# Mask addition and row maxima of a graph-attention kernel: one DVE instruction for each head, with negated scores

## The reference, cut to what is computed

```python
bias = jnp.where(adj_matrix > 0, 0.1 * edge_attr_matrix * adjf, -jnp.inf)[:, None]
scores = jnp.einsum('bhqd,bhkd->bhqk', q, k) / np.sqrt(HD) + bias
attn = jax.nn.softmax(scores, axis=-1)
out = jnp.einsum('bhqk,bhkd->bhqd', attn, v)
...
x1 = residual + (out @ wo + bo)
mlp = jax.nn.gelu(n2 @ w1 + b1, approximate=False) @ w2 + b2
...
for k in range(L):                                   # L = 2 layers
    scores = jnp.einsum('bof,bif->boi', q, kk) / SCALE
    scores = jnp.where(mask, -10000000000.0, scores)
    attn = jax.nn.softmax(scores, axis=2)
    attn = jnp.where(mask, 0.0, attn)
    ctx = jnp.einsum('bnd,ed->bne', jnp.einsum('boi,bid->bod', attn, x), Wc[k])
    x = layer_norm(x + ctx, ln_g[k], ln_b[k])
```

## Time and profile before

| | |
|---|---|
| median of 3 runs | 2197.3 us (2193.87 to 2198.27) |
| the profiled execution | 2195.11 us, of which its span is 2193.1 us |
| granted TensorE clock, mean of the span | 0.971 |
| PE busy | 2016.2 us (92%) |
| PEld busy | 1499.2 us (68%) |
| DVE busy | 1721.4 us (78%) |
| ACT busy | 1558.7 us (71%) |
| POOL busy | 961.0 us (44%) |
| chain that ended last, by engine | PE 72%, ACT 13%, DVE 6%, POOL 4% |

### The profile page before, as it was taken

The page is one execution under the profiler, slowest core; times in us unless marked ns, Lnnn a source line. Parts: engine busy times, 40 slices in busy tenths (PEclk is TensorE's granted clock), DMA queues, the critical chain, the costliest instruction groups (busy, mean ns, idle before and its releaser), DMA issues.

```text
span 2193.1 us, 45905 instructions
## 1 busy us (share of the span) xinstructions
PE 2016.2 (92%) x16984; PEld 1499.2 (68%) x16984; DVE 1721.4 (78%) x3397; ACT 1558.7 (71%) x2994; POOL 961.0 (44%) x1304
## 2 busy tenths in 40 slices
PE   5589899999999999999999999999999999999853
PEld 4356677777777777777777777777777777777531
DVE  4566788888888888888888888888888888887422
ACT  2367777777788777777787777777877777777521
POOL 2022344445454454444554544445545444544434
PEclk8799999999999999999999999999999999999976
DMA  3211012222211122222111222222111222210000
GB/s 106 73 49 42 28 45 58 59 59 56 58 49 42 33 59 59 59 59 54 49 42 35 57 58 59 59 54 57 43 39 44 59 59 59 54 50 16 15 10 19
DMA packets 103675, 108.62 MB, mean 50 GB/s; under 512 B 9824, under 2 KB 78432, under 8 KB 103456
## 3 DMA queue, kind: packets, MB, share of 16 engines
q1 hardware_dynamic: 102912, 104.90, 17.9%
q0 software_dynamic: 544, 0.80, 0.2%
HBM read 38.55 MB, written 16.78 MB: 25 GB/s over the span
## 4 chain that ended last, share of the span: by engine, by line
PE 72%; ACT 13%; DVE 6%; POOL 4%; issue 3%; DMA 2%; SPq 1%; DVEq 0%; POOLq 0%; ACTq 0%
PE ps L243 18%; PE ps L245 17%; PE ps L244 17%; PE ps L812 5%; PE ps L972 5%; PE ps L1046 5%; ACT area L483 4%; PE ps L1026 3%; POOL x L403 3%; ACT cs L525 2%; DMA out<-x 2%; ACT area L533 2%; ACT L525 2%; PE ps L965 1%; ACT cq L518 1%
## 5 line engine op out<-in xcount | busy, mean ns | idle before, releaser
L483 ACT ACTIVATE area<-area,nmax 128x128 f32<-128x128 f32 x1024 | 312.5, 390 | 0.8
L243 PE MATMUL ps<-w_h,hid_h 128*128 128x256 f16 x1024 | 279.1, 273 | 6.0 <-POOL hid_l L250 5.1
L245 PE MATMUL ps<-w_h,hid_l 128*128 128x256 f16 x1024 | 279.0, 272 | 0.0
L244 PE MATMUL ps<-w_l,hid_h 128*128 128x256 f16 x1024 | 279.0, 272 | 0.0
L396 POOL TENSOR_TENSOR ve<-mv,eps_cols 128x4 f32<-128x4 f32 x128 | 25.7, 201 | 572.0 <-DVE mv L572 572.0
L250 POOL TENSOR_TENSOR hid_l<-area,hid_h 128x512 f16<-128x512 f32 x128 | 151.8, 1186 | 251.9 <-ACT hid_h L506 251.9
L503 ACT ACTIVATE area<-ps,b_col 128x512 f32<-128x512 f32 x256 | 176.3, 689 | 77.9 <-PE ps L245 76.8
L403 POOL TENSOR_TENSOR x<-xh,cg_row 128x256 f32<-128x256 f32 x128 | 89.0, 728 | 295.7 <-DMA out<-x 272.6
L243 PE MATMUL ps<-rot_h,w_h 128*128 128x512 f16 x512 | 194.4, 380 | 6.2 <-ACT area L503 2.9
L245 PE MATMUL ps<-rot_h,w_l 128*128 128x512 f16 x512 | 194.0, 379 | 0.0
L244 PE MATMUL ps<-rot_l,w_h 128*128 128x512 f16 x512 | 193.9, 379 | 0.0
(11 more groups left out here) (178 smaller groups left out, 6214.0 us busy)
## 6 DMA issues: line engine op xcount, KB each, us to landing
qkS<-qk SPq DMA_DIRECT2D x384, 128.0 KB, 2.4
xin<-in_x SPq DMA_DIRECT2D x32, 512.0 KB, 3.8
adj_in<-in_adj SPq DMA_DIRECT2D x64, 256.0 KB, 2.9
out<-x SPq DMA_DIRECT2D x32, 512.0 KB, 3.9
area<-in_L_gnn_w SPq DMA_DIRECT2D x2, 1024.0 KB, 11.3
area<-in_L_gnn_Wc SPq DMA_DIRECT2D x2, 256.0 KB, 11.3
area<-in_L_gnn_wq SPq DMA_DIRECT2D x1, 256.0 KB, 3.7
area<-in_L_gnn_wk SPq DMA_DIRECT2D x1, 256.0 KB, 4.0
```

Of the source, the lines that this page charges most:

```text
L243: pe.matmul(dst, lh, rh, start=start, stop=False, **kw)
L244: pe.matmul(dst, lh, rl, start=False, stop=False, **kw)
L245: return pe.matmul(dst, ll, rh, start=False, stop=stop, **kw)
L483: last = act.activation(sc[:, b % 2, h], sc[:, b % 2, h], ACT.Exp, bias=nmax[:, b, h:h + 1])
```

## The change

The two DVE steps S and max become one. For each head of A (8 for a graph) and for each graph of C (4 for a layer) DVE issues one instruction that adds the bias to the scores, multiplies by a negative constant, writes the result, and keeps the running minimum of what it wrote. The minimum of the negated scores is the negated maximum that ACT needs; ACT reads the negated scores with scale -1. The steps A.max and C.max leave VECTOR, all else in the lists stays where it was. The semaphores d_max and d_cmax are gone: ACT waits for d_S and d_cS, and these are counted behind the last head. The edge term of biasA is scaled by QK_SCALE ahead, since the addition now comes before the scaling. The line numbers of the changed kernel are one or two higher than those of the kernel before.

```diff
-           "A.wo-1", "A.st-1", "A.S0+0", "C1.S-4", "C1.max-4", "A.xh-1", "A.max0+0", "N.st+1",
+           "A.wo-1", "A.st-1", "A.S0+0", "C1.S-4", "A.xh-1", "N.st+1",
...
-                        need(act, d_max, g, B, b + 1)
+                        need(act, d_S, g, B, b + 1)
                         for h in range(H):
                             last = act.activation(sc[:, b % 2, h], sc[:, b % 2, h], ACT.Exp,
-                                                  bias=nmax[:, b, h:h + 1])
+                                                  bias=nmax[:, b, h:h + 1], scale=-1.0)
...
-                            need(act, d_cmax[l], g, 1, 1)
+                            need(act, d_cS[l], g, 1, 1)
...
-                        dve.scalar_tensor_tensor(adj_f, adj_in[:, :, :], 0.1, adj_in[:, :, :],
+                        dve.scalar_tensor_tensor(adj_f, adj_in[:, :, :], 0.1 * QK_SCALE, adj_in[:, :, :],
...
-                        dve.scalar_tensor_tensor(sc[:, b % 2], psA_heads, 1.0 / QK_SCALE,
-                                                 biasA[:, b].unsqueeze(1).broadcast_to([P, H, P]),
-                                                 ALU.mult, ALU.add).then_inc(d_S, 1)
-                    elif stage == "A" and what[:3] == "max":
-                        need(dve, d_S, g, B, b + 1)
-                        dve.tensor_reduce(nmax[:, b, :], sc[:, b % 2], AX.X, ALU.max, negate=True).then_inc(d_max, 1)
+                        for h in range(H):
+                            last = dve.tensor_tensor_reduce(sc[:, b % 2, h], psA_heads[:, h], biasA[:, b],
+                                                            scale=-1.0 / QK_SCALE, scalar=HIGHEST,
+                                                            op0=ALU.add, op1=ALU.min,
+                                                            accum_out=nmax[:, b, h:h + 1])
+                        last.then_inc(d_S, 1)
...
-                            dve.tensor_tensor(cs[:, l], psC_S, biasC[:, g[1]], ALU.add).then_inc(d_cS[l], 1)
-                        elif what == "max":
-                            need(dve, d_cS[l], g, 1, 1)
-                            dve.tensor_reduce(cmax[:, l], cs[:, l], AX.X, ALU.max, negate=True).then_inc(d_cmax[l], 1)
+                            for b in range(B):
+                                last = dve.tensor_tensor_reduce(cs[:, l, b], psC_S[:, b], biasC[:, g[1], b],
+                                                                scale=-1.0, scalar=HIGHEST, op0=ALU.add,
+                                                                op1=ALU.min, accum_out=cmax[:, l, b:b + 1])
+                            last.then_inc(d_cS[l], 1)
```

More of the change, by code:

```diff
@@ L44 @@
 MASKED = -1e30
+HIGHEST = 3e38
 P_SCALE = 1024.0
@@ L64 @@
 VECTOR = ["Q.k1+0", "A.AV2-1", "A.PT3-1", "A.AV3-1", "C1.xT-4", "A.oT-1", "C0.PV-3", "M.x2-2",
[2 rows of a table removed]
+          "A.wo-1", "A.st-1", "A.S0+0", "C1.S-4", "A.xh-1", "N.st+1",
+          "Q.v1+0", "M.mT-1", "A.S1+0", "M.mC-2", "N.xh+1", "M.lo0-1", "C1.PV-4",
           "A.PT0+0", "C1.st-4", "N.xT+1", "Q.v0+0", "C1.xh-4", "M.lo2-1", "A.S2+0", "C0.xT-2",
[2 rows of a table removed]
+          "Q.k0+1", "C0.st-3", "M.lo4-1", "A.PT1+0", "Q.q0+1", "A.S3+0", "C0.S-2",
+          "A.AV0+0", "M.lo6-1", "Q.q1+1", "Q.mA+1", "A.PT2+0", "C0.xh-3",
           "A.AV1+0"]
@@ L207, in graph_blocks @@
         d_mt, d_mA, d_mC = sem("d_mt"), sem("d_mA"), sem("d_mC")
-        d_S, d_max = sem("d_S"), sem("d_max")
+        d_S = sem("d_S")
         d_PT, d_rec, d_o, d_oT, d_x1 = (sem("d_" + n) for n in ("PT", "rec", "o", "oT", "x1"))
         d_mT, d_lo, d_x2 = (sem("d_" + n) for n in ("mT", "lo", "x2"))
-        d_cT, d_cS, d_cmax = (each_layer("d_" + n) for n in ("cT", "cS", "cmax"))
+        d_cT, d_cS = (each_layer("d_" + n) for n in ("cT", "cS"))
         d_crec, d_csc, d_cy = (each_layer("d_" + n) for n in ("crec", "csc", "cy"))
@@ L521, in iteration @@
                         elif what == "ex":
-                            need(act, d_cmax[l], g, 1, 1)
+                            need(act, d_cS[l], g, 1, 1)
                             for b in range(B):
                                 last = act.activation(cs[:, l, b], cs[:, l, b], ACT.Exp,
-                                                      bias=cmax[:, l, b:b + 1],
+                                                      bias=cmax[:, l, b:b + 1], scale=-1.0,
                                                       accum_out=csum[:, l, b:b + 1])
```

## The result

The changed kernel takes 2200.2 us (2196.7 to 2204.9, 20 runs), the kernel before 2197.2 us (2193.4 to 2199.4, 20 runs) beside it. The ratio is 1.0015, 95% interval 1.0008 to 1.0022: 3 us slower, and within the 0.2% that the prediction called no change. It had forecast 2260 us and 2215 to 2330. The profiled execution of the changed kernel has a span of 2196.3 us, that of the kernel before 2193.1.

A forecast was written before the change was run, and what follows sets the result against it. PE was taken as the bound, losing 2.03 us a period to later bank release: 57 us in the steady part plus 8 at the ends, 65 us on 2195.1, giving 2260 us. Range for 8 in 10: 2215 to 2330.

The forecast's parts named there:

- no change: Rival: PE's stalls hide in something taken for PE-bound that isn't; 2199 us, chance 0.04. Any result within 0.2%: 0.07.
- What bounds the kernel: Steady part: PE is the bound, busy 60.96 of 62.0 us; DVE matters only through when PE's banks are released.
- the term of A.PT1: PE's A.PT1, waiting for A.S2 on DVE, late by 8p - 1.44 = 0.80 us a period.
- three terms: Later bank release for PE: 12p - 2.31 at C1.xW, 8p - 2.06 at A.PT0, 8p - 1.44 at A.PT1.
- The view of the waits: Steady part: PE's idle time is all named by three ACT waits of 0.38, 0.27 and 0.23 us a period.
- The cost of a pair: On DVE, distance p between starts of successive pairs: first half 0.20 plus minimum's read 0.08, p = 0.28 us.
- 28p - 5.81: Lateness of PE summed over the three places, 2.03 us a period, all lost; 57 us over the steady part.
- A.PT0: PE late by 8p - 2.06 = 0.18 us a period, on top of the exps wait; M.mT on DVE not late.
- C1.xW: PE's first matmul into bank 6, waiting for C1.S on DVE, late by 12p - 2.31 = 1.05 us a period.
- DVE's total: DVE's load hardly moves, 0.2 us a period less at p = 0.28, and isn't the bound: 0.
- Filling and emptying: Both ends of the run: later A.S0, A.PT1 and C.S waits cost about 8 us, bounds 0 to 14.
- short pair: Rival on DVE: p from 0.19 to 0.24, the read hiding beside the next first half; 2206 to 2229 us, chance 0.13.

The follow-up runs named there:

- e4: Changed kernel with A.S2 on DVE moved ahead of C1.xh and M.lo2; 2193.7 us, ratio 0.9986 to the kernel before.
- e9: Changed kernel with a two-column DVE copy out of PSUM behind each pair; 2249.9 us, ratio 1.0248 to the kernel before.
- e8: Changed kernel with six series of 8 DVE instructions ahead of its loop, to time pairs and plain instructions alone; 2209.0 us in one run.
- e2: Kernel before with the change in stage A only, graph layers keeping their addition and max; 2193.5 us, ratio 0.9987.
- e3: Kernel before with the change in the graph layers only, stage A keeping its addition and max; 2187.7 us, ratio 0.9958.
- e6: Kernel before with the copy of C1.xW moved from ACT to DVE; 2211.1 us, ratio 1.0059.
- e7: Changed kernel with C1.xW's copy on DVE and A.S2 ahead of C1.xh; 2184.3 us, ratio 0.9939 to the kernel before.
- e5: Changed kernel with the copy of C1.xW moved from ACT to DVE; 2189.4 us, ratio 0.9968 to the kernel before.
- e1b_pad: Changed kernel with a short DVE addition of two SBUF scratch tiles behind each pair; 2465.9 us, ratio 1.1221 to the kernel before.

## Why the prediction was wrong

**What bounds the kernel: right.** PE is the bound, and what the change costs is the later release of its banks. e4 removes the term of A.PT1 by moving DVE's step, and e9 makes all three terms grow as the formula says. "The view of the waits names all of that idle time" was too much: it left out two delays of 0.23 us (M.up0) and 0.07 (C1.PV).

**The cost of a pair: this step failed.** It stands under "What a pair costs": "The second half: ... I take 0.08, between the two. p = 0.28 us." The first half was put at 0.20, and that is right (the pair's 0.21 less the 0.01 of e8's series). The second half was put at 0.08 and measured 0.01 at most, so the pair measured 0.211 us in place of 0.28. The argument was that tiny DVE instructions are 0.07 us apart and that ACT's read costs 0.09. Neither carries over: the read's record has the same start as the next first half, and the distance is that of a plain instruction. The sum 28p - 5.81 is so steep that this one term decides it. At 0.211, with its zero at A.PT0, the formula gives 0.47 us a period instead of 2.03, and 13 us instead of 57.

The Trainium skill's "Vector Engine (DVE) Microarchitecture Reference", section 5.2, had pointed the same way as the rows: it led to an estimate of 0.284 us a pair; the measured distance is 0.211, and the trace decides. Section 7 of that page of the Trainium skill, a half rate for a related form with two SBUF sources, was weighed as a rival. Here two fp32 sources in SBUF ran as fast as one from PSUM, 0.21 us (e8). The rule of the Trainium skill is for another form than this one, and no run here tests it.

**The size of the three terms: right for their p.** With p = 0.279 put in by hand (e9) the three places are late by 1.04, 0.17 and 0.77 us against 1.04, 0.17 and 0.79 from the formula, and the kernel takes 2249.9 us. With p = 0.211 C1.xW has +0.21 against +0.22 and A.PT1 +0.23 against +0.25.

**A.PT0: right in sum, wrong in its ground.** M.up0 had a small wait for M.mT on DVE, too short for the view of waits: DVE's step ended at 1042.90 + 1.22 = 1044.12, and PE's timeline has M.up0 right behind it, 0.72 us after the start of C1.PT (1043.54); in the changed kernel it is 0.49 (1044.92 to 1045.41). The row of the kernel before, then the two of the changed one:

```profile
1044.26 0.38 PE L243 MATMUL ps<-rot_h,w_h 128*128 128x512 f16 x1
```

```profile
1044.92 0.66 PE L1039 MATMUL ps<-ident,cs 128*128 128x128 f32 x4 [0.27 <-ACT area L534]
...
1045.41 0.38 PE L244 MATMUL ps<-rot_h,w_h 128*128 128x512 f16 x1
```

DVE gets to M.mT earlier now, so M.up0 wins 0.23 us; but the exps of graph 0 on ACT end no earlier, so A.PT0 waits 0.23 longer. The gain is turned into a longer wait for ACT. The prediction had put M.mT on DVE as not late, and missed that it had been late before.

**DVE's total: "hardly moves" was wrong with p.** 8 pairs take 1.69 us where S and max took 2.26, and DVE's busy time in the window falls from 53.3 to 49.5 us. The prediction gave this no value, as DVE wasn't the bound. It probably had one after all, on a detour: the steady part is 4.6 us longer where the three terms at their measured sizes give 0.21 + 0.23 = 0.44 us a period, 12 us. M.down7 (-0.17) and C1.PV (-0.07) give 6 us back. PE waited at M.down7 for GpSimd in some periods, by up to 1.2 us; the groups of POOL, 290 us to the end of the steady part, show that GpSimd itself waits less for the output's DMA (first before, then changed):

```profile
L403 POOL TENSOR_TENSOR x<-xh,cg_row 128x256 f32<-128x256 f32 x108 | 75.2, 728 | 270.9 <-DMA out<-x 270.9
```

```profile
L404 POOL TENSOR_TENSOR x<-xh,cg_row 128x256 f32<-128x256 f32 x108 | 75.4, 730 | 250.8 <-DMA out<-x 250.8
```

In SP's list the store stands behind the load that waits for DVE's bias preparation, and this ends some 0.7 us earlier relative to A.wo in the changed kernel. That chain (DVE, SP, DMA, GpSimd, PE) is read from the traces; no experiment took it alone, so it isn't shown. For it speaks that e2 and e3 have the gain too, each with a part of DVE's work gone (-0.21 and -0.17), while e6, with more work on DVE, loses there (+0.12).

**Filling and emptying: +8 expected, -1.6 measured.** At p = 0.211 the prediction's terms for the two ends come to 3 to 4 us and not 8. The five waits for C.S near the end grew by its formula, from 0.79 to 1.03 us (4p + 0.08 - 0.69 = 0.23). What gave this back in the emptying part, and more, is the granted clock: windows of the two kernels at the same place, before first (us, busy of the engines, granted clock, DMA, GB/s):

```profile
2119.00:2134.00 15.00, 10.46 (x51) 5.95 (x50) 3.38 (x8) 4.05 (x11) 0.20 (x1) 0.76 0.00 1
```

```profile
2124.50:2137.00 12.50, 7.72 (x51) 4.93 (x49) 2.93 (x14) 4.05 (x11) 0.42 (x1) 1.00 0.01 2
```

The same 51 matmuls run wholly at the 2.4 GHz level in the changed kernel and in part at the 1.2 GHz level before: PE is busy 7.72 us with them and not 10.46. In e3, with the filling part's clock at 0.85 over its first 145 us against 0.81, the filling part is 3 us shorter. These are single executions, and no run shows what moved the clock, so differences of this size at the ends aren't put down to the change here. Why the filling part of the changed kernel is 1.1 us shorter at the same clock (0.81) stays open.

**The rivals.** The measured p is that of the "short pair" (0.19 to 0.24), which had a chance of 0.13 and 2206 us as its lower end. At p = 0.211 it gives 2195 + 13 + 4 = 2212; what lies between this and the 2200 measured are the gains at M.down7 and C1.PV (6 us) and the two ends (6 us). So the right p alone would still have forecast a slower kernel, and that no change came out is in part luck. By its number the result is nearest "no change" (2199 us, chance 0.04), but not by the way there: PE's stalls don't hide, since e9 loses at all three places what the formula says. The two sides for p, 0.13 and 0.43, held the truth; but the weight lay on the middle, where 0.58 were given to 0.24 to 0.32 with the reason that the two engines overlap alike. With a slope of 28 periods x 28 = 784 us for each us of p, 0.07 us are 55 us as long as all three terms are above zero (44 here, as A.PT0's ends at p = 0.26). A price with no row of its own, times such a slope, should have had a range that reaches the no-cost case, near 2206, with more than 0.13.

## What to carry to other kernels

When one wide instruction is replaced by many short ones, work out the slope first: how much time one nanosecond of the short one is worth. If that decides the sign, measure a series of them alone before anything else; e8's series would have given p. And where a change takes load off an engine which isn't the bound, look for what can use the room: this change alone is 0.15% slower, with the copy moved and A.S2 earlier (e7) it is 0.6% faster, and e5's edit cost 0.6% before the change and won 0.5% behind it.

## What the runs showed of the hardware

- DVE's read of an accumulator costs next to nothing between the starts of its neighbours: pairs 0.21 us apart at 128 columns and 0.11 at 32, plain instructions 0.01 us less (e8_micro). On ACT the read costs 0.09 us a pair.
- A DVE instruction of two columns with SBUF as its only source takes 0.55 us instead of 0.15 while GpSimd works on 128 x 256 tiles (e1b_pad); with PSUM as its source it stays at 0.15 (e9_pad_ps). All 355 slowed ones in e1b_pad end 0.02 us behind the end of a GpSimd instruction, whose own length is 0.72 us. Some 11 of the 40 pads a period were slowed, and the kernel is some 215 us longer than with the PSUM pads (2465.9 against 2249.9). The new pairs, with one source in PSUM, aren't slowed. Whether pairs with both sources in SBUF would be wasn't tried beside GpSimd.
- In the emptying part, where PE idles often (7.72 us busy of a window of 12.5), the same 51 matmuls had a granted clock of 0.76 in one kernel and 1.00 in the other, and kept PE busy for 10.46 or 7.72 us. What tips it wasn't tried.
